# Layer-0 attention on one Trainium2 core: two units' sums in the halves of one PSUM bank, and a third bank for turned probabilities

## What is computed

```python
q = q.reshape(b, l, KVH, GROUPS, HD).transpose(0, 2, 3, 1, 4)
k = k.reshape(b, s, KVH, HD).transpose(0, 2, 1, 3)
v = v.reshape(b, s, KVH, HD).transpose(0, 2, 1, 3)
scores = jnp.einsum('bkgld,bksd->bkgls', q, k) * scale
scores = scores + encoder_attention_mask[:, :, None, :, :]
attn = jax.nn.softmax(scores, axis=-1)
out = jnp.einsum('bkgls,bksd->bkgld', attn, v)
```

## Times and profile before

| | us |
|---|---|
| median of 3 runs | 2770.42 |
| the three runs | 2774.18, 2765.03, 2770.42 |
| the profiled execution's own time | 2769.69 |
| its span, first to last instruction | 2767.9 |

### The profile page before, as it was taken

The page is one execution under the profiler, slowest core; times in us unless marked ns, Lnnn a source line. Parts: engine busy times, 40 slices in busy tenths (PEclk is TensorE's granted clock), DMA queues, the critical chain, the costliest instruction groups (busy, mean ns, idle before and its releaser), DMA issues.

```text
span 2767.9 us, 50324 instructions
## 1 busy us (share of the span) xinstructions
PE 2654.8 (96%) x17432; PEld 2135.9 (77%) x17432; DVE 1724.6 (62%) x2626; ACT 1515.7 (55%) x2360; POOL 1323.8 (48%) x750
## 2 busy tenths in 40 slices
PE   6899999999999999998978999999999999999989
PEld 5577678888878888886856776788888888888867
DVE  5799775665556565564157996765656566556541
ACT  4788744455545455544447886545555455555443
POOL 2332335466634566644423232456665346665643
PEclk9999999999999999999989999999999999999999
DMA  7311114444522544442463101245354224453512
GB/s 202 92 40 33 64 28 122 106 117 102 134 75 56 120 104 116 125 104 69 168 126 89 33 32 64 47 104 130 93 129 111 71 71 116 103 133 97 131 54 73
DMA packets 87731, 261.94 MB, mean 95 GB/s; under 512 B 19696, under 2 KB 33280, under 8 KB 81168
## 3 DMA queue, kind: packets, MB, share of 16 engines
q1 hardware_dynamic: 87568, 259.80, 35.9%
HBM read 135.45 MB, written 6.83 MB: 51 GB/s over the span
## 4 chain that ended last, share of the span: by engine, by line
issue 35%; PE 29%; POOL 29%; DMA 2%; DVE 2%; SPq 1%; ACT 1%; POOLq 1%; DVEq 0%; ACTq 0%
POOL pT L463 16%; PE ps_t L1058 9%; POOL wa L463 5%; PE ps_m L1073 4%; PE ps_m L938 4%; POOL v L463 4%; PE ps_s L1045 4%; PE ps_s L938 3%; POOL wo L463 2%; PE ps_t L938 2%; PE ps_m L1111 1%; DMA scr_q<-parts 1%; SPq L341 1%; DMA acc<-in_rows 1%; PE ps_m L1176 1%
## 5 line engine op out<-in xcount | busy, mean ns | idle before, releaser
L463 POOL TENSOR_TENSOR pT<-pT,pT 128x1024 fp32r<-128x1024 f32 x224 | 538.8, 2406 | 511.1 <-ACT pT L628 510.5
L628 ACT ACTIVATE pT<-pT 128x1024 fp32r<-128x1024 f32 x224 | 237.8, 1062 | 359.2 <-DMA pT<-pb 359.2
L754 ACT ACTIVATE p<-ps_s,nm 128x1024 f32<-128x1024 f32 x256 | 284.5, 1111 | 257.1 <-DVE nm L1554 256.9
L938 PE MATMUL ps_s<-kT,qT 128*128 128x512 f32 x1536 | 394.7, 396 | 9.9 <-ACT p L754 5.3
L1570 DVE STREAM_TRANSPOSE pb<-p 128x1024 f32<-128x1024 f32 x224 | 278.3, 1243 | 112.3 <-ACT p L754 102.7
L938 PEld LDWEIGHTS ps_s<-kT,qT 128*128 128x128 f32 x1536 | 279.6, 188 | 80.2 <-ACT p L754 18.6
L1551 DVE TENSOR_REDUCE nmx<-ps_s 128x1 f32<-128x1024 f32 x256 | 309.4, 1209 | 43.3 <-PE ps_s L938 43.2
L1481 DVE CUSTOM_DVE_ANT_0 sm<-ps_s,mask 128x1024 f32<-128x1024 f32 x256 | 309.7, 1210 | 12.1 <-PE ps_s L1045 10.7
L708 ACT ACTIVATE p<-sm,nm 128x1024 f32<-128x1024 f32 x256 | 293.4, 1146 | 38.4 <-DVE nm L1481 27.5
L1058 PEld LDWEIGHTS ps_t<-ident,p 128*128 128x128 f32 x2048 | 225.4, 143 | 91.7 <-issue 72.1
L1058 PE MATMUL ps_t<-ident,p 128*128 128x128 f32 x2048 | 287.0, 284 | 6.3 <-ACT pt L628 3.2
(11 more groups left out here) (137 smaller groups left out, 4153.0 us busy)
## 6 DMA issues: line engine op xcount, KB each, us to landing
pT<-pb SPq DMA_DIRECT2D x896, 128.0 KB, 2.4
stg_qk<-in_wqk SPq DMA_DIRECT2D x40, 1024.0 KB, 7.5
stg_vo<-in_wo SPq DMA_DIRECT2D x48, 512.0 KB, 3.5
wob<-in_wo SPq DMA_DIRECT2D x32, 512.0 KB, 3.5
stg_vo<-in_wv SPq DMA_DIRECT2D x32, 512.0 KB, 3.6
q_stack<-scr_q SPq DMA_DIRECT2D x48, 128.0 KB, 4.3
st_ctx<-in_ctxT SPq DMA_DIRECT2D x8, 512.0 KB, 5.5
mask<-in_mask SPq DMA_DIRECT2D x2, 2048.0 KB, 12.6
```

The source lines that it names most:

```text
L463: return nc.gpsimd.tensor_tensor(out, x, f32(hi), ALU.subtract)
L628: return nc.scalar.activation(out, in_, ACT.Copy)
L754: nc.scalar.activation(p[t % 2][:], ps_s[t % 2][:], ACT.Exp, bias=nm[:, i:i + 1], scale=SCALE1, accum_out=sums[:, i:i + 1]).then_inc(exp_d ...
L938: mm = nc.tensor.matmul(out, lhs(x, c), rhs(y, c), start=start and c == 0 and i == 0, stop=stop and c == n_tiles - 1 and i == 2)
```

## The change

The halves of all steps of a batch are numbered h = 2t + q. The first 16 (the first unit) go to `ps_t[0]` and `ps_t[1]` by turns as before. From h = 16 on they go round three banks, `ps_t[0]`, `ps_t[1]` and `ps_m[1]`. A half waits for the copy of the last half that used its bank. The sums of unit u now lie in `ps_m[0]`, at column 0 for even and column 256 for odd units, and the turned inverses 128 columns behind them. The first value matmul of unit u waits for `a0_done` of unit u-1, where it was unit u-2. The output projection begins with `ps_m[1]` instead of `ps_m[0]`.

```diff
+        turn_banks = [*ps_t, ps_m[1]]
+        bank_of_half = [h % 2 if h < 2 * UNIT else h % 3 for h in range(2 * STEPS0)]
+        def half0(t, q):
+            return turn_banks[bank_of_half[2 * t + q]]
+        def half_before(t, q):
+            h = 2 * t + q
+            return next((divmod(k, 2) for k in reversed(range(h)) if bank_of_half[k] == bank_of_half[h]), None)
+        def unit0(u):
+            return ps_m[0][:, u % 2 * 2 * P:u % 2 * 2 * P + P]
+        def inverse0(u):
+            return ps_m[0][:, u % 2 * 2 * P + P:u % 2 * 2 * P + 2 * P]
...
                 def turned0(t):
                     pe.wait_ge(exp0_done, t0 + t + 1)
                     for q in range(2):
-                        if t >= 1:
-                            pe.wait_ge(t0_copied[q], t0 + t)
+                        before = half_before(t, q)
+                        if before is not None:
+                            pe.wait_ge(t0_copied[before[1]], t0 + before[0] + 1)
+                        elif bank_of_half[2 * t + q] == 2:
+                            pe.wait_ge(bank_free, nb + U_PROJ0 + 2)
                         for s in range(4):
                             st = 4 * q + s
-                            mm = nc.tensor.transpose(ps_t[q][:, s * P:(s + 1) * P],
+                            mm = nc.tensor.transpose(half0(t, q)[:, s * P:(s + 1) * P],
...
-                    if e == 0 and i == 0 and u >= 2:
-                        pe.wait_ge(a0_done, u0 + u - 1)
+                    if e == 0 and i == 0 and u >= 1:
+                        pe.wait_ge(a0_done, u0 + u)
...
-                            mm = nc.tensor.matmul(ps_m[u % 2][gr * 2 * HD:(gr + 1) * 2 * HD, 0:P],
+                            mm = nc.tensor.matmul(unit0(u)[gr * 2 * HD:(gr + 1) * 2 * HD, :],
...
-                        mm = nc.tensor.matmul(ps_m[lt % 2][:], aT0[:, c, lt * P:(lt + 1) * P], w0o[:, c, :],
+                        mm = nc.tensor.matmul(ps_m[(lt + 1) % 2][:], aT0[:, c, lt * P:(lt + 1) * P], w0o[:, c, :],
```

More of the change, by code:

```diff
@@ L715, in copied0 @@
                     act.wait_ge(t0_filled[q], t0 + t + 1)
-                    copy(pt0[t % RING][:, 4 * q:4 * q + 4, :], ps_t[q][:].rearrange("p (s n) -> p s n", s=4))\
+                    copy(pt0[t % RING][:, 4 * q:4 * q + 4, :], half0(t, q)[:].rearrange("p (s n) -> p s n", s=4))\
                         .then_inc(t0_copied[q], 1)
@@ L729, in _ @@
                         act.wait_ge(rb0_filled, b * UNITS0 + u + 1)
-                        copy(rb0[u % 2][:], ps_m[u % 2][:, P:2 * P]).then_inc(rb0_done, 1)
+                        copy(rb0[u % 2][:], inverse0(u)).then_inc(rb0_done, 1)
                 act.wait_ge(rb0_filled, b * UNITS0 + UNITS0)
-                copy(rb0[1][:], ps_m[1][:, P:2 * P]).then_inc(rb0_done, 1)
+                copy(rb0[1][:], inverse0(UNITS0 - 1)).then_inc(rb0_done, 1)
                 act.wait_ge(row_added, b * ROWS + 2)
@@ L1079, in values0 @@
                         pe.wait_ge(r0_done, u0 + u + 1)
-                        nc.tensor.transpose(ps_m[u % 2][:, P:2 * P], r0[u % 2][:].rearrange("p h d -> p (h d)"),
+                        nc.tensor.transpose(inverse0(u), r0[u % 2][:].rearrange("p h d -> p (h d)"),
                                             ident[:]).then_inc(rb0_filled, 1)
@@ L1489, in copied0 @@
                     nc.vector.tensor_copy(pt0[t % RING][:, 4 * q:4 * q + 4, :],
-                                          ps_t[q][:].rearrange("p (s n) -> p s n", s=4)).then_inc(t0_copied[q], 1)
+                                          half0(t, q)[:].rearrange("p (s n) -> p s n", s=4)).then_inc(t0_copied[q], 1)
                 def inverse(u):
@@ L1500, in normalised @@
                     dve.wait_ge(rb0_done, u0 + u + 1)
-                    nc.vector.tensor_tensor(aT0[:, kp, lt * P:(lt + 1) * P], ps_m[u % 2][:, 0:P], rb0[u % 2][:],
+                    nc.vector.tensor_tensor(aT0[:, kp, lt * P:(lt + 1) * P], unit0(u), rb0[u % 2][:],
                                             ALU.mult).then_inc(a0_done, 1)
@@ L1523, in add_out @@
                     dve.wait_ge(bank_filled, n0 + lt + 1)
-                    nc.vector.tensor_tensor(x_res[:, lt, :], ps_m[lt % 2][:], x_res[:, lt, :], ALU.add)\
+                    nc.vector.tensor_tensor(x_res[:, lt, :], ps_m[(lt + 1) % 2][:], x_res[:, lt, :], ALU.add)\
                         .then_inc(bank_free, 1)
```

## The result

| | before | after |
|---|---|---|
| median | 2770.59 us, 6 runs | 2746.48 us, 6 runs |
| lowest to highest | 2765.03 to 2774.85 | 2743.34 to 2748.18 |
| span of the profiled execution | 2767.9 us | 2743.8 us |

The ratio is 0.9915, with a 95% interval from 0.9905 to 0.9925: 24 us faster. The forecast was 2747.

A forecast was written before the change was run, and what follows sets the result against it. The prediction took PE, 96% busy, to bound the kernel, with 0.20 us lost per 3.99 us cycle. Its terms, 22.4 + 0.4 = 22.8 us, taken from 2769.69 gave 2746.9, named as 2747, range 2741 to 2759.

The forecast's parts named there:

- The two losses: PE's odd turn in the first attention: 0.13 us lost before it and 0.07 inside it, per cycle of two steps.
- Part 1: Turned halves in three banks: both waits of the odd turn go, 0.20 us per cycle (bounds 0.07 and 0.20), cycle 3.79.
- the half-clock rows: Profile rows at half clock: two scores take 0.85 to a turn, 0.99 to values, so only values pay a switch.
- the first rival: A switch to the turn still costs 0.08 at full clock: 13.4 us saved, about 2757; chance 0.15.
- the second: Rival: the 0.13 before the odd turn isn't ACT's, only 0.07 goes: 7.8 us saved, about 2762; chance 0.07.
- The last rival: PE packs closer without waits, DVE bounds the cycle at 3.58 us: 46 us saved, about 2724; chance 0.02.
- Part 2: Cycle count: odd steps 15 to 125, 56 turns of 0.20, 11.2 us per batch, 22.4 in all; steps 9, 11 nothing.
- Part 3: Tail, step 127's turn, which stood 0.49 us for ACT's copy: 0.2 us per batch (bounds 0 and 0.5), 0.4 together.
- Part 4: ACT and DVE keep up with a cycle of 3.79: spare 0.34 and 0.29 us per cycle; PE is late next.
- Part 5: First values of a new unit wait for the unit before's normalisation: met 0.68 us ahead, cost zero.
- The rival: The shared bank's wait decides at each unit's first value matmul: PE stands 1.07 us at 30 units, about 2779; chance 0.05.
- The sum: Whole kernel: 22.4 + 0.4 = 22.8 us saved; 2769.69 - 22.8 = 2746.9, for a median 2747.

## Why the prediction was right

- **The bound.** PE full of starts, with 0.20 us of loss in a cycle of 3.99. The two losses were in the pieces that the rows gave, and both went: 0.57 to 0.43 and 0.95 to 0.88. The thirteen units without the third bank took 208.51 us, so nothing else in the change did it.
- **Part 1, the term of 0.20.** The cycle is 3.78 for 3.79. The choice between 0.07 and 0.20 rested on the half-clock rows, that scores pass to a turn without a gap. They do at full clock too, 0.43, while scores to values stays 0.52. So no switch remains, as the first rival had it, and the 0.13 was ACT's, against the second: with the third bank for first halves alone it went too. The sustained spacing of about 81 ns for 128 columns in the Trainium skill ("TensorE: Matmul & The Clock Gate", section "Back-to-back issue gap") was not reached even with no wait left: a turn is 0.88 / 8 = 0.11 us per transpose. The last rival, closer packing, did not come.
- **Part 2, the count.** The thirteen units gave 10.61 us: 52 cycles of 0.20, and 0.2 from a late copy (below). What steps 9 and 11 won did not count, though the stand's length alone doesn't show it: 10.43 and 9.51 us before, 10.05 and 10.57 after. POOL's first row work, which waits for a transfer, began 35.12 and 34.59 us behind the batch's first scores before, 34.52 and 34.90 after. The inverses' transpose came 40.2 and 39.7 behind the same scores, then 39.6 and 40.0. It moved as POOL's work moved, 0.6 earlier in batch 1 and 0.3 later in batch 2, and not as PE's turns did.
- **Part 3, the tail.** Mis-sized a little. From the inverses of unit 14 to those of unit 15 it went from 319.60 to 328.74, 9.14, to 308.83 to 317.47, 8.64. One odd turn's 0.20 apart, that is 0.3 per batch for 0.2.
- **Part 4, ACT and DVE.** 6.8 and 7.9 us of waiting left, for "about 9" and "about 7". They keep up, and PE is what is late next. One time was off, at no cost: DVE's copy for the odd turn at 112.73 was put at 114.19, a period before 118.18. In the trace of the kernel before it begins at 114.39, with the normalisation ahead of it, and it is done 1.5 us before the bank is wanted at 116.59 all the same.
- **Part 5, the new wait.** 0.67 us ahead for 0.68. The two kernels with a later normalisation show what the number was worth. The rival wanted it to decide once the normalisation came 1.4 us later: 1.13 later the kernel was still 11 us faster than before, 1.74 later it was 7 us slower, where the rival had named 9.
- **The sum.** 22.8 us was counted. From the first scores to the last inverses the two stages took 275.9 and 275.8 us and take 263.6 and 263.5: 24.6 us less. The 1.8 beyond the sum are terms that it had not. The late copy gives 0.2 per batch and the tail 0.1. The stretch before the inverses of unit 0 became 0.6 shorter in one batch and 0.3 longer in the other, with POOL's transfer. Unit 1 became 0.7 and 1.5 us shorter, where its three odd turns at full clock explain 0.6.

The 0.9 that is left in unit 1 of batch 2 is the clock. The granted clock was 0.50 up to 1476.7 before, 5.6 us behind the inverses' transpose at 1471.11. After, it was 0.50 up to 1463.4, 3.7 us behind the one at 1459.71:

```profile
1462.54 1.05 PE L1081 MATMUL ps_m<-ident,p 128*128 128x128 f32 x4
1463.39 0.63 PE L1081 MATMUL ps_t<-ident,p 128*128 128x128 f32 x4
1463.86 0.60 PE L1065 MATMUL ps_s<-k_stack,q_stack 96*128 96x512 bf16 x2
1464.38 1.08 PE L1096 MATMUL ps_m<-pt,v 128*32 128x128 f32 x32
```

The odd turn takes 1.32 where the earlier trace rows have 1.71, and scores to values 0.52 where they have 0.99: 0.86 us. In batch 1 the clock came back 4.7 us behind the transpose before and 4.6 after. No run ties the time at which it comes back to the change, so it is counted as chance here and not as part of the mechanism.

The mechanism was right, and the closeness of the time was partly luck. The prediction took its 22.8 from the profiled execution and named 2747 for the median; from the median that it had, 2770.42, the same sum gives 2747.6. The change was worth 24.1 us by the medians, 21 to 26 by the interval, and over 1 us of the stages' 24.6 is the clock and the transfer.

The profile after, the kernel without the third bank, and the two with half of it show the mechanism.

## What to carry to other kernels

When an engine reads as full, compare the spacing of the starts with what the same instructions take where nothing holds them; a wait of a tenth of a microsecond per step hides in the busy time. When a step is released by two engines, find when each of them releases it: taking away one wait alone may be worth nothing. And when two buffers move into one bank, the price is the cover of the new wait, which can be read from the timeline before it is paid.

## What was not expected

Once per batch the kernel before had a scores-to-turn spacing of 0.84 in place of 0.57. The row of the kernel before:

```profile
213.11 1.06 PE L1058 MATMUL ps_t<-ident,p 128*128 128x128 f32 x8 [0.25 <-ACT pt L628]
```

ACT's copy came late there: it began 1.03 us behind the start of the even turn, where the earlier trace rows have 0.76. What held it is not known. Unit 8 took 16.25 us for it, where the other units took 16.02. In the changed kernel all 104 such spacings in the steady units are 0.43 to 0.44. So a spare bank also hides a single late copy, here 0.23 us. With the bank for second halves alone the 0.84 is there again, with the bank for first halves it is not, as it should be if the copy is ACT's.

The stand for POOL at the end of unit 0 was taken as given. Moving POOL's row work behind the inverses was worth 21 us alone (2770.7 to 2750.0), nearly as much as the change itself, and both together give 2722.2 and 2720.6, the fastest kernel of this study.
